# A local-attention transformer on one core: row sums moved from ScalarE's accumulator to VectorE, evacuations moved to ScalarE, and another order of work in the attention steps

## What is computed

```python
def attn_layer(x, Wqkv, qs, ksc, Wo):          # 16 heads of 64, windows of 32 tokens
    q, k, v = split(x @ Wqkv)
    q = l2norm(q) * qs;  k = l2norm(k) * ksc
    q = q * cos * scale + rotate_half(q) * sin * scale
    k = k * cos * inv + rotate_half(k) * sin * inv
    sim = einsum(q, k of this window and the one before) * 8, masked
    return (softmax(sim) @ v) @ Wo
...
for i in range(6):
    x = attn_layer(shift_tokens(x), ...) + x
    x = ffn_layer(shift_tokens(x), ...) + x
```

## Time and profile before

| | |
|---|---|
| time, median of 3 runs | 3575.65 us (3574.94 to 3576.36) |
| time of the profiled execution | 3575.57 us |
| its span in the profile | 3573.7 us |
| mean granted clock of PE | 0.958 of full speed |
| busy shares | PE 91%, PEld 62%, DVE 78%, ACT 82%, POOL 57% |

### The profile page before, as it was taken

One profiled execution on the slowest core, in us unless ns is written; L12 is line 12 of the kernel. 1 busy time (PEld: TensorE's weight loads), 2 busy tenths in 40 slices (PEclk: granted clock), 3 DMA queues, 4 the chain that ended last, 5 costly groups with the idle time before them and its releaser, 6 DMA issues. The chain is left out here.

```text
span 3573.7 us, 118257 instructions
## 1 busy us (share of the span) xinstructions
PE 3252.6 (91%) x42076; PEld 2208.0 (62%) x42076; DVE 2791.6 (78%) x5370; ACT 2933.6 (82%) x9257; POOL 2045.7 (57%) x2150
## 2 busy tenths in 40 slices
PE   5699998889999789999789999978999977999977
PEld 4466665656666556666566666665666655666656
DVE  7788887578888568888658888757888856888865
ACT  3399998479999459999649999937999955999973
POOL 3566665456666356666446666545666634666644
PEclk8799999899999899999899999989999989999999
DMA  2000001100000100000110000010000010000011
GB/s 70 10 7 8 7 7 33 22 13 7 7 7 6 47 15 8 7 7 7 37 24 7 8 7 7 10 44 14 7 8 7 6 43 19 8 7 7 7 34 42
DMA packets 141061, 57.58 MB, mean 16 GB/s; under 512 B 118598, under 2 KB 137668, under 8 KB 139460
## 3 DMA queue, kind: packets, MB, share of 16 engines
q1 hardware_dynamic: 140484, 50.01, 5.9%
HBM read 22.57 MB, written 2.10 MB: 7 GB/s over the span
## 5 line engine op out<-in xcount | busy, mean ns | idle before, releaser
L1321 ACT ACTIVATE probs<-s_ps,nbias,rnorm 128x64 f32<-128x64 f32 x3072 | 1229.9, 447 | 1.6 <-DVE nbias L1039 0.9
L1524 POOL TENSOR_TENSOR qk_rot<-by_cos,by_sin 128x1024 f32<-128x1024 f32 x384 | 914.0, 2380 | 381.9 <-DVE by_sin L989 334.8
L597 PE MATMUL ring<-wvo,xsT 128*32 128x512 f32 x6144 | 794.8, 600 | 10.2 <-ACT vo L1144 10.2
L1321 ACT ACTIVATION_READ_ACCUMULATOR probs<-s_ps,nbias,rnorm 128x1 f32 x3072 | 765.0, 249 | 0.0
L1513 POOL TENSOR_TENSOR probs<-probs,rrow 128x256 f32<-128x256 f32 x768 | 454.6, 613 | 429.1 <-DVE rrow L973 429.1
L986 DVE TENSOR_TENSOR by_cos<-qk_ps,rotary 128x1024 f32<-128x1024 f32 x378 | 463.0, 1225 | 147.1 <-ACT squares L1307 147.1
L1533 POOL TENSOR_TENSOR qk_rot<-qk_rot,rnorm 128x1024 f32<-128x1024 f32 x192 | 365.5, 1904 | 341.4 <-DVE rnorm L733 341.4
L543 PEld LDWEIGHTS ring<-cst,qk_rot 128*128 128x128 f32 x3072 | 341.3, 141 | 243.7 <-ACT vo L1144 155.9
L543 PE MATMUL ring<-cst,qk_rot 128*128 128x128 f32 x3072 | 446.4, 278 | 27.6 <-POOL qk_rot L1524 24.4
L1001 DVE TENSOR_REDUCE sumsq<-squares 128x16 f32<-128x1024 f32 x384 | 462.9, 1206 | 0.0
L989 DVE TENSOR_TENSOR by_sin<-qk_ps,rotary 128x1024 f32<-128x1024 f32 x378 | 459.2, 1215 | 0.0
(11 more groups left out here) (166 smaller groups left out, 5433.4 us busy)
## 6 DMA issues: line engine op xcount, KB each, us to landing
qk_rot<-L_ffn_Wqkv SPq DMA_DIRECT2D x7, 1024.0 KB, 5.1
xs<-x_tok SPq DMA_DIRECT2D x194, 32.0 KB
xs<-x_tok SPq DMA_DIRECT2D x194, 31.8 KB
by_cos<-x_tok SPq DMA_DIRECT2D x48, 128.0 KB
by_cos<-x_tok SPq DMA_DIRECT2D x48, 127.0 KB
wv<-L_ffn_Wqkv SPq DMA_DIRECT2D x7, 512.0 KB, 6.6
wo_pad<-L_ffn_Wo SPq DMA_DIRECT2D x14, 256.0 KB, 7.3
xs<-x_tok SPq DMA_DIRECT2D x194, 0.2 KB
```

The costliest lines, as they stand in the source:

```text
L597: last = mm(r[WIN * mh:WIN * (mh + 1), :], xsT[:, a, WIN * w:WIN * (w + 1)], wvo[:, mh, :, :], start=True, stop=True)
L1321: last = nc.scalar.activation(probs[:, a, h // 4, :, h % 4, :], s_ps[:, half, c:c + 2 * WIN].rearrange("p (s c) -> p s c", s=2), ACT.Exp, ...
L1524: g.tensor_tensor(qk_rot[:, n, :], by_cos[:, n, :], by_sin[:, n, :], ALU.add).then_inc(added[qk], 1)
```

## The change

1. The exponentials lose the accumulator. ACT's second instruction to each of them goes, and DVE takes the row sums instead (`row_sums`, one reduction over 128 x 512 for each half of the heads). The exponentials of a half now stand together, eight in a row.
2. DVE's two evacuations to a step (one of k, one of values) go to ACT.
3. Each engine's order in a step is new. The output comes at stage 4 where it was 3, scores and transposes of some halves one stage later, and a layer's pipeline has NT + 4 steps in place of NT + 3. `RING_USES` follows: the output is in bank 0, where the tokens' transpose (`xsT`) was before it.

```diff
-        RING_USES = (("xsT", 0), ("qT0", 1), ("vo3", 2), ("vo1", 1), ("o", 3), ("vo2", 1), ("vo0", 1), ("kT0", 1),
+        RING_USES = (("o", 4), ("qT1", 2), ("kT0", 2), ("vo0", 2), ("vo2", 2), ("kT1", 2), ("pT0", 3), ("qT0", 1),
...
+                    def row_sums(half, s):
...
+                        T, a, h = T0 - s, (par - s) % 2, slice(8 * half, 8 * half + 8)
+                        dve.wait_ge(exp_done[half], done(T))
+                        p = probs[:, a, 2 * half:2 * half + 2].rearrange("p q s h c -> p q h s c")
+                        v.tensor_reduce(psum_row[:, h].rearrange("p (q h) -> p q h", q=2), p, AXY,
+                                        ALU.add).then_inc(row_summed[half], 1)
...
-                        for h in (h0, h0 + 1):
+                        for h in range(4 * quad, 4 * quad + 4):
...
-                                scale=rnorm[:, a, h:h + 1], bias=nbias[:, h:h + 1],
-                                accum_out=psum_row[:, h:h + 1])
+                                scale=rnorm[:, a, h:h + 1], bias=nbias[:, h:h + 1])
...
-                    vo_evacuated(2, 1)
-                    residual(3)
...
+                    residual(4)
+                    sum_of_squares("q", 1)
+                    rotate("k", 0, 1)
+                    row_reciprocals(1, 3)
+                    rotate("k", 1, 1)
+                    sum_of_squares("k", 1)
+                    maxima(0, 2)
                     xsT_lower(0)
...
-                every_tile(step, 3)
+                every_tile(step, 4)
```

More of the change, by code:

```diff
@@ L31 @@
 AX = mybir.AxisListType.X
+AXY = mybir.AxisListType.XY
 P = 128
@@ L316, in schedule, with every_tile @@
                 step(k, k % 2, None)
-        def every_tile(step, depth, before_last=None):
+        def every_tile(step, depth, at=None, begun=None):
             for k in range(NT + depth):
-                if before_last and k == NT + depth - 1:
-                    before_last()
+                if k == at:
+                    begun()
                 step(k)
@@ L618, in output @@
                         last.then_inc(o_ps, 1)
+                    output(4)
+                    transposed("q", 1, 2)
+                    project("k", 0, 1)
+                    project("k", 1, 1)
+                    transposed("k", 0, 2)
+                    values(0, 2)
+                    values(2, 2)
+                    transposed("k", 1, 2)
+                    scores(0, 2)
+                    probs_transposed(0, 3)
+                    transposed("q", 0, 1)
                     xs_transposed(0)
-                    transposed("q", 0, 1)
                     scores(1, 2)
-                    values(3, 2)
                     project("q", 0, 0)
                     project("q", 1, 0)
+                    probs_transposed(1, 3)
+                    values(3, 2)
                     values(1, 1)
[L627 to L637, removed]
-                every_tile(step, 3)
+                every_tile(step, 4)
                 pe.wait_ge(x_mid, done(NT * l + NT - 1))
@@ L933, in copy @@
                         return v.tensor_copy(out_, in_)
[L935 to L955, removed]
                     def xsT_lower(s):
@@ L1069, in step @@
                         variance4(1, 1)
-                    row_reciprocals(1, 2)
-                    k_evacuated("low", 0, 1)
-                    sum_of_squares("q", 0)
-                    rotate("k", 0, 0)
-                    maxima(0, 1)
-                    rotate("k", 1, 0)
-                    softmax_bias(0, 1)
                 def lower(u, par):
@@ L1117, in step4 @@
                     x_new(u)
-                every_tile(step, 3, before_last=lambda: normalised(0, 0))
+                every_tile(step, 4, NT + 3, lambda: normalised(0, 0))
                 dve.wait_ge(b1_in, 96 * l + 96)
@@ L1326, in exponentials @@
-                        if h0 % 8 == 6:
+                                scale=rnorm[:, a, h:h + 1], bias=nbias[:, h:h + 1])
+                        if quad % 2:
                             last.then_inc(exp_done[half], 1)
+                    p_evacuated(1, 4)
+                    xsT_evacuated(1)
+                    exponentials(2, 3)
+                    exponentials(3, 3)
+                    vo_evacuated(3, 3)
+                    vo_evacuated(1, 2)
+                    q_evacuated(1, 2)
@@ L1329, in step @@
+                    square("k", 1)
+                    k_evacuated("low", 0, 2)
+                    k_evacuated("high", 0, 2)
+                    vo_evacuated(0, 2)
+                    k_evacuated("low", 1, 2)
+                    k_evacuated("high", 1, 2)
+                    vo_evacuated(2, 2)
                     xsT_upper(0)
                     q_evacuated(0, 1)
+                    p_evacuated(0, 3)
                     exponentials(0, 2)
-                    exponentials(2, 2)
-                    exponentials(4, 2)
```

64 lines of the change are left out of this document (27 added, 37 removed).

## The result

The changed kernel takes 3674.85 us (median of 4 runs, 3669.89 to 3676.62) against 3575.3 us; the ratio is 1.0276, with a 95% interval from 1.0258 to 1.0294. It is slower by 99 us, 17 us a layer. I had forecast 3685.

A forecast was written before the change was run, and what follows sets the result against it. PE was taken to bound the kernel. Per layer, steps +19.6, fill -0.7 and end -0.8 + 0.2 made +18.3 us; six layers, +110 on 3575.6, gave 3685 us, range 3583 to 3760.

The forecast's parts named there:

- 28 steps: A layer's full steps between token transposes: each 14.73 us, 0.70 more than 14.03, so +19.6 us a layer.
- fill: A layer's start up to the fourth token transpose, steps without output: 37.3 us against 38.0, so -0.7.
- end of attention: Last token transpose to last k normalised: 20.6 us against 21.4, so -0.8; the last residual adds 0.2.
- The exponential: Spacing of ACT's exponentials without accumulator reads: one every 0.29 us.
- The chain, 5.75 us: Token transpose through bias, eight exponentials, square and two copies to the output: 5.75 us; PE alone 5.28, waiting 0.47.
- PE's order, +0.23: PE's own least step: one more pair of tiling changes, 0.30, less a 0.07 wait, giving 14.26 us.
- the remainder of the step: PE's step from the output to the next token transpose: 14.26 - 5.28 = 8.98 us.
- PE stays the bound, 3592: Rival: exponentials under 0.23 us, no wait at the output, step 14.26, 3592 us; chance 0.17.
- Shorter: Rival: exponentials under 0.23 us and tiling changes under 0.07 a pair, step 13.96, 3541 us; chance 0.12.
- A further wait: Rival: costly DVE row sums or POOL's late k addition delaying the exponentials; 3770 us at +0.5 a step; chance 0.11.

The follow-up runs named there:

- e6: The kernel before, old order and evacuations, with row sums by VectorE and eight exponentials of 128x128 in place of sixteen; 3575.4 us, ratio 1.000.
- e7: The kernel before with the second value projection moved between the k transposes and k projections, adding one pair of tiling changes a step; 3623 us.
- e4: The changed kernel with eight exponentials of 128x128, two heads at a time, in place of sixteen of 128x64; 3602 us.
- e8: The changed kernel with the output off the token copy's bank (3659 us) and GpSimd's sum of rotated k held until the second softmax bias; 3664.61 us.
- e2: The changed kernel with the accumulators back and no row sums on VectorE; 3867 us.
- w1: The kernel before with both score halves behind the token transpose, half 0's maxima and bias at VectorE's step start, first q transposes behind the q projections; 3980 us.
- e1: The kernel before with no accumulator, row sums by VectorE and all evacuations by ScalarE, in the old order of work; 3606.56 us.
- w4: The kernel before with the third value projection moved behind the q projections; 3720.66 us.
- w3: The kernel before with VectorE row sums, both score halves at the step's end, GpSimd's sum of k held, two exponentials ahead of xsT_hi; 3595.7 us.

## Why the prediction was right

The sum per layer, forecast and measured:

| Term | forecast | measured |
|---|---|---|
| 28 steps | 28 x 0.70 = +19.6 | 406.0 - 392.9 = +13.1 |
| fill | -0.7 | 42.6 - 38.0 = +4.6 |
| end of attention | -0.8 + 0.2 | (1201.69 + 1.90 - 1183.8) - 21.4 = -1.6 |
| layer | +18.3 | +17.0 |

The layer's total comes from one first token transpose to the next layer's, so it holds what the three terms leave out, 0.9 us.

The mechanism was right at its centre. PE was the bound (e6, e7) and ACT's relief bought nothing by itself; the output waits for ACT's token copy; the wait is ACT's chain (e4 takes it away and with it 73 us). Three terms were mis-sized, and it was luck that two of the errors cancelled.

**The exponential** was forecast at 0.29 us behind the one before and is 0.29. The estimate from the figures of the Trainium skill ("ScalarE: Activation LUTs", section "What ACT_TABLE_LOAD costs") was 0.33, with 57 us more; the measurement decides against it.

**The chain, 5.75 us**, is 5.55. I let the exponentials start at 1.55 behind DVE's bias and POOL's sum, whose end I placed at 1.35. It ends at 1.23 (892.66 + 2.38 - 893.81), and they start at 1.44, and e8 shows what holds them: ACT's three copies. My figure of 1.49 for these was the link that counts. Another 0.09 lies behind the token copy. These 0.20 us are most of the 0.23 that the step came out shorter.

**PE's order, +0.23** (0.30 for a pair less 0.07), is +0.11 in e4 with the chain out of the way, though the pair alone costs 0.25 (e7); what makes up the rest was not looked for. It had no part in the step, since the output waits; only the remainder of the step, 8.98 forecast and 893.81 - 884.90 = 8.91 measured, goes by it.

**The fill, 37.3 us**, is the step that failed. I took spacings from the middle of a layer and got 9.6 + 13.3 + 14.4; measured are 12.2 + 14.7 + 15.7. The timeline of the changed kernel shows two things in the fill that no such row has:
```profile
735.52 1.28 ACT L1137 ACT_TABLE_LOAD   x1 [3.19 <-issue]
```
```profile
769.64 0.47 PE L530 MATMUL qk_ps<-wqk_hi,xsT_hi 128*128 128x512 f32 x1 [1.82 <-DVE by_sin L978]
...
770.61 0.63 PE L530 MATMUL qk_ps<-wqk_hi,xsT_hi 128*128 128x512 f32 x1
771.04 0.63 PE L531 MATMUL qk_ps<-wqk_lo,xsT_hi 128*128 128x512 f32 x1
771.46 0.63 PE L532 MATMUL qk_ps<-wqk_hi,xsT_lo 128*128 128x512 f32 x1
```
A table load of 1.28 us ahead of ACT's first copy (the kernel before has one at its place too, of the same length), and projections 0.43 us apart where they are 0.23 apart in a full step. Windows over the three intervals, then the third interval in e4; the granted clock is the number behind POOL's busy time:
```profile
735.20:747.40 12.20, 6.64 (x17) 4.82 (x18) 6.01 (x7) 3.78 (x5) 2.35 (x1) 0.67 0.11 18
747.40:762.10 14.70, 11.94 (x88) 6.18 (x86) 10.98 (x18) 7.58 (x13) 7.73 (x4) 0.81 0.03 6
762.10:777.80 15.70, 13.82 (x132) 7.96 (x132) 11.95 (x24) 12.63 (x30) 9.72 (x8) 0.89 0.03 6
...
749.70:763.30 13.60, 12.21 (x131) 7.07 (x132) 11.34 (x24) 10.86 (x22) 8.80 (x8) 1.00 0.03 7
```
PE pauses in the fill (1.82 us in the row above) and runs part of each interval at 1.2 GHz, half its clock. In the kernel before this holds for the first two intervals (granted clock 0.55 and 0.79, in 7.6 and 15.9 us) and not for the third (1.00, in 14.5), so both things could have been read ahead of the forecast. The price of the drop in the third interval shows inside the changed kernel: five layers have it (0.89) and take 15.6 to 15.7 us, while the fourth layer has the same pause of 1.83 us, keeps 1.00 and takes 14.1. So the pause alone doesn't bring the drop; what does was not found. In e4 the interval takes 13.6, at full clock and with the shorter exponentials.

Against the kernel before, the fill's growth lies in its first interval (12.2 for 7.6 us), where the second token transpose now stands behind transposes of q that wait 3.5 us for POOL's sum; the forecast had that as 9.6. In all the fill is 5 us longer than forecast, and the full steps are 0.23 x 28 = 6.4 us shorter. That these two nearly cancel is why 3685 was near.

**The rivals.** *PE stays the bound, 3592*: its condition was an exponential under 0.23 us. e4 makes it true by force, and gives 3602. *Shorter*: no. *A further wait*: the row sums are cheap (0.68 long), and POOL's sum of k meets L1007 but holds back the exponentials in few steps. It was a real danger all the same: e2 and w1 show what it costs when it falls on the chain.

**How the 99 us divide.** By e4, 73 us are ACT's chain with its fill, and 27 are left for all else; PE's own order, 0.11 x 168 = 19 us, is within these. In the old order the first two parts of the change cost 31 us, most of it by way of POOL's queue (e1); whether that path still has a share in the 27 was not separated.

## What to carry to other kernels

Relieving an engine, even by 3.3 us a step (e6), buys nothing where another one's queue bounds the step, but an order that puts its work in one block makes a chain of it: three copies, eight exponentials, a square and two copies in a row, with the bounding engine waiting at the end. Before moving an instruction in the bounding engine's queue, list what its semaphore releases as well as what it waits for: w4 lost 145 us, by its trace through a buffer that the moved projection was the last to read. Count changes of tiling around the whole step, not at one place: w3 and w4 were built on a saving that the count doesn't have. And size the fill by rows of the fill, not of a full step: its clock and its pauses are others.

## What the runs showed of the hardware

**GpSimd's sum holds up some operations of VectorE and not others.** In w1, a bias of 8 columns with both inputs in SBUF takes 1.83 us beside GpSimd's sum of two SBUF tensors and ends with it; with the sum held back it takes 0.17, and 302 us are won. It leaves other operations alone. Timeline of w1, GpSimd's sum and a rotation that reads one input from PSUM:
```profile
890.59 2.37 POOL L1532 TENSOR_TENSOR qk_rot<-by_cos,by_sin 128x1024 f32<-128x1024 f32 x1 [0.16 <-PE ring L543]
...
891.15 1.22 DVE L994 TENSOR_TENSOR by_cos<-qk_ps,rotary 128x1024 f32<-128x1024 f32 x1 [0.28 <-ACT squares L1315]
```
The rotation keeps its 1.22 us. The Trainium skill ("SBUF — State Buffer", section "Who interferes with whom") says that a VectorE instruction with two SBUF inputs contends with a GpSimd one that reads SBUF, that one with at most one SBUF input outside the two-port modes does not, and that who issues first has the pair for its whole instruction. The traces agree: 1.83 us against 1.22, though the two rows differ in the operation as well as in the operand. By it, that the scalar operation L1007 is held as well (0.45, 0.74, and 0.17 in e8) would be a two-port mode; no run here shows which mode it used.

**A change between products of 128 and of 32 columns costs TensorE about 0.12 us**, an estimate: half of e7's 0.25 a pair.
